# Transposing quantised activations as pairs in fp32 words, in the feed-forward phase of a decoder layer

## The chip, the core and the metric

The kernel runs on one core of one Trainium2 chip. The metric is the device time of one execution in microseconds; a kernel is given by the median of several runs.

## The reference

A decoder layer on 16 sequences of 128 tokens and 1024 channels: causal attention with rotary positions (16 heads of 64), a convolution over three neighbouring columns weighted by cosine similarities of a context, and a feed-forward part, each with a residual and a layer norm behind it. The feed-forward part is quantised: activations to integers from -128 to 127 by the row's maximum, weights to -1, 0 and 1 times a mean; its inner width is 2752.

```python
def _act_quant(x):
    scale = 127.0 / jnp.clip(jnp.max(jnp.abs(x), axis=-1, keepdims=True), EPS)
    xq = jnp.clip(jnp.round(x * scale), -128.0, 127.0) / scale
    return x + jax.lax.stop_gradient(xq - x)
...
    gate = jax.nn.silu(_bitlinear(x, w_gate))
    up = _bitlinear(x, w_up)
    return _bitlinear(gate * up, w_down)
x = _layernorm(x + _L0_attn_ref(x, L0_attn_w_q, L0_attn_w_k, L0_attn_w_v, L0_attn_w_out), axis=-1)
x = _layernorm(x + _L0_xattn_ref(x, ctx_4096, L0_xattn_weight), axis=-1)
x = _layernorm(x + _L0_ffn_ref(x, L0_ffn_w_gate, L0_ffn_w_up, L0_ffn_w_down), axis=-1)
```

## The kernel before

The kernel works in two phases, each with one turn per sequence. Phase 1 does the attention and turns the feed-forward weights into ternary fp8 values, which it stores in a DRAM scratch (`tern_dram`). Phase 2 (`turn2` of every engine) does the convolution and the feed-forward part. Between them, in phase 1's last turn, SP loads the ternary weights (lines 432 to 441): `gate8` and `up8` as 8 tiles of 128 input channels by 2752, `down8` as 22 tiles of 128 inner channels by 1024. All engines run their own hand-written order and meet at semaphores.

A turn i of phase 2, by TensorE's order (lines 711 to 747):

- The gate and up products (L717): 6 chunks of up to 512 columns, 8 matmuls for gate and 8 for up in each. The stationary operand is `xqT`, the integers of x, with channels on the partitions. ACT applies silu (L972), VectorE multiplies (L1454) and takes maxima (L1447) into `hbuf`.
- The convolution of the next sequence, 18 matmuls (L542).
- The transposes of h (L733), 22 tiles in bf16 by `idb`, in four groups `HT_USES` that take turns in two PSUM banks. h is rounded before them: ACT and VectorE add `MAGIC` to the scaled values (L978, L1466), VectorE takes it away again, limits to 127 and writes bf16 (L1472, four quarters). VectorE then evicts each group with a limit at -128 into `hT` (L1481). A group in a bank waits for the eviction of the group before it in that bank (`trh_free`).
- The down product (L745), 22 pairs of matmuls. It waits for the first two evictions before tile 0 and for the last two before tile 12. Before tile 19 come the transposes of the next x (L552), 8 tiles in bf16, which VectorE evicts into `xqT` (L1150).
- The next turn begins when `xqT` is there (`pair_free[1]`, line 712).

VectorE's order after the second eviction of h: the residual of the next x (L1133), its norm's sums (L1089 to L1094), the last two evictions of h, the norm itself (L1099), maximum and scale of x (L1082 to L1142), then, when ACT has rounded x (L784), the integers (L1146) and the eviction of `xqT` (L1150). Then it finishes the output y of this turn (L1489, L1089, L1099).

Transposes in phase 1 (L503) are in fp32 by `idf`. In the trace's names, the buffers of phase 2 are part of `weights`, and the integers of x lie in `rope_c`, y in `k`.

Of the kernel before, what the change touches and what calls it, by code (L numbers as in the profile page):

```python
# [7 lines left out]
P = 128  # L8
B, S, D = 16, 128, 1024
H, HD = 16, 64  # L10
KT = D // P
I = 2752
IT = -(-I // P)
# [28 lines left out]
HT_USES = ((0, 6), (6, 12), (12, 17), (17, 22))  # L42
HQ_NEEDS = [-(-min(hi * P, I) * 4 // I) for _, hi in HT_USES]

# [35 lines left out]
def decoder(nc, x, xT_in, ctx, wqT, wkT, wvT, woT, w_ffn, conv_w, cos, sin, causal, ident, out):  # L80
# [4 lines left out]
    with ExitStack() as stack:  # L85
# [10 lines left out]
        idb = sb("idb", [P, P], BF16)  # L96
# [31 lines left out]
        down8 = w8[:, 2 * KT * I:2 * KT * I + IT * D].rearrange("p (k n) -> p k n", k=IT)  # L128
        hbuf = over(over_out, I)
        hq = over(over_out, IT * P // 2).bitcast(BF16)  # L130
# [59 lines left out]
        xq = rope_c[:].bitcast(BF16)  # L190
# [163 lines left out]
        def _(sp):  # L354
# [38 lines left out]
            def turn(b, mode, has_next, has_next2):  # L393
# [29 lines left out]
                if has_next:  # L423
                    if not (isinstance(b, int) and b == 0):

                        sp.wait_ge(x1_stored, b * 16)
                    sp.dma_start(xres, x[bass.ds(b, 1)].rearrange("o s d -> s (o d)")).then_inc(xres_loaded, 16)
                else:

                    for w in range(2):  # L430
                        sp.wait_ge(pj_full[w], pj_uses(B - 1, 5) + 1)
                    for m, w8m in enumerate((gate8, up8)):
                        src = tern_dram[m * WCH:(m + 1) * WCH].rearrange("r p n -> (r p n)").rearrange("(k p n) -> p k n", p=P, n=I)
                        for t in (0, 4):
                            sp.dma_start(w8m[:, t:t + 4].bitcast(U8), src[:, t:t + 4]).then_inc(ffn_in, 16)
                    src = tern_dram[2 * WCH:3 * WCH].rearrange("r p n -> (r p n)").rearrange("(i n) -> i n", n=D)
                    full = (IT - 1) * P
                    src_t = src[0:full].rearrange("(k p) n -> p k n", p=P)
                    for lo, hi in ((0, 7), (7, 14), (14, IT - 1)):
                        sp.dma_start(down8[:, lo:hi].bitcast(U8), src_t[:, lo:hi]).then_inc(ffn_in, 16)  # L440
                    sp.dma_start(down8[0:I - full, IT - 1].bitcast(U8), src[full:I]).then_inc(ffn_in, 16)
# [55 lines left out]
        def _(pe):  # L497
# [48 lines left out]
            def xq_T(n, uses):  # L546
# [3 lines left out]
                bank = ps[:, 2].bitcast(BF16)  # L550
                for t in range(KT):
                    ins = nc.tensor.transpose(bank[:, t * P:(t + 1) * P], xq[:, t * P:(t + 1) * P], idb[:])  # L552
# [156 lines left out]
            def turn2(i, has_next):  # L709
# [16 lines left out]
                for u, (lo, hi) in enumerate(HT_USES):  # L726
# [4 lines left out]
                    bank = ps[:, TH + w].bitcast(BF16)  # L731
                    for t in range(lo, hi):
                        ins = nc.tensor.transpose(bank[:, (t - lo) * P:(t - lo + 1) * P], hq[:, t * P:(t + 1) * P], idb[:])  # L733
# [255 lines left out]
        def _(dve):  # L989
# [154 lines left out]
            def integers_x(n):  # L1144
                dve.wait_ge(x_rounded, n + 1)
                nc.vector.tensor_scalar(xq, xrnd, MAGIC, 127.0, ALU.subtract, ALU.min).then_inc(xq_ready, 1)  # L1146

            def xqT_out(uses):
                dve.wait_ge(pair_full[1], uses + 1)
                nc.vector.tensor_scalar(xqT, ps[:, 2].bitcast(BF16).rearrange("p (t n) -> p t n", n=P), -128.0, None,  # L1150
# [272 lines left out]
            nc.vector.tensor_copy(idb[:], idf[:]).then_inc(set_up, 1)  # L1423
# [19 lines left out]
            def turn2(i, has_next):  # L1443
# [23 lines left out]
                for a in range(4):  # L1467
# [4 lines left out]
                    nc.vector.tensor_scalar(hquarter(a, hq), hquarter(a), MAGIC, 127.0, ALU.subtract, ALU.min) \  # L1472
                        .then_inc(hq_ready, 1)
                for u, (lo, hi) in enumerate(HT_USES):
# [5 lines left out]
                    src = ps[:, TH + w].bitcast(BF16)[:, 0:(hi - lo) * P].rearrange("p (t n) -> p t n", n=P)  # L1480
                    nc.vector.tensor_scalar(hT[:, lo:hi], src, -128.0, None, ALU.max).then_inc(trh_free[w], 1)  # L1481
# [22 lines left out]
        def _(pool):  # L1504
# [31 lines left out]
            def turn(b, mode, has_next, has_next2):  # L1536
# [7 lines left out]
                if not has_next:  # L1544
# [3 lines left out]
                    nc.gpsimd.memset(down8[64:P, IT - 1], 0.0).then_inc(padded, 1)  # L1548
# [99 lines left out]
```

## Time and profile before

| | us |
|---|---|
| median of 3 runs | 1415.58 |
| lowest, highest | 1411.53, 1416.8 |
| profiled execution | 1411.78 |
| its span, first to last instruction | 1410.0 |
| TensorE busy (matmul) | 1365.8 |
| VectorE busy | 1056.1 |
| ScalarE (ACT) busy | 623.7 |
| GpSimd (POOL) busy | 217.0 |

The profile is of one execution. PE is TensorE's matmul row and PEld its weight loads, DVE is VectorE, SPq a queue of DMA issues. Busy shares are averages over both phases; phase 2 begins at 851 us. Matmuls are pipelined, so the ends of matmuls are modelled, and the starts are the ones to compare.

### The profile page before, as it was taken

The numbers are of one execution on the slowest core, as the hardware profiler recorded it, in microseconds if no ns is written. First come the engines' busy times: TensorE is split into PE (matmuls) and PEld (weight loads), VectorE is DVE, ScalarE is ACT, GpSimd is POOL, SyncE is SP. The second block draws the span as 40 slices with busy tenths as digits, with TensorE's granted clock in tenths as the row PEclk, the third lists the DMA queues.
The fourth block names the chain that finished last, engine by engine and source line by source line (L and its number), as shares of the span: only waits on it lengthen the run. The fifth ranks groups of instructions, "written<-read, shape, count | busy, mean of one in ns | idle before, by whom it ended". The sixth has DMA issues, their size and how long they took to land. (4 is left out here: it accounts for less than half of the span.)

```text
span 1410.0 us, 23306 instructions
## 1 busy us (share of the span) xinstructions
PE 1365.8 (97%) x7560; PEld 690.9 (49%) x7560; DVE 1056.1 (75%) x1851; ACT 623.7 (44%) x1209; POOL 217.0 (15%) x262
## 2 busy tenths in 40 slices
PE   8889999999999999999999989999999999999996
PEld 3344555545545554554554544444444444444443
DVE  4996456446577777868867768888888888888884
ACT  7876474455455545545544542332222232223221
POOL 0003213121131321312222221000000000000000
PEclk9999999999999999999999999999999999999999
DMA  9515454445435354453443583222222222222200
GB/s 375 223 61 181 137 186 143 168 132 182 142 111 177 137 160 141 147 178 113 159 159 124 134 278 111 76 75 74 74 74 74 74 74 74 74 74 74 77 27 16
DMA packets 63732, 178.92 MB, mean 127 GB/s; under 512 B 15392, under 2 KB 26832, under 8 KB 63696
## 3 DMA queue, kind: packets, MB, share of 16 engines
q1 hardware_dynamic: 63696, 178.48, 39.2%
q8 instruction: 18, 0.29, 0.1%
q14 instruction: 18, 0.15, 0.0%
HBM read 153.02 MB, written 25.43 MB: 127 GB/s over the span
## 5 line engine op out<-in xcount | busy, mean ns | idle before, releaser
L512 PE MATMUL ps<-weights,xT 128*128 128x512 f16 x2112 | 472.7, 381 | 7.0 <-ACT v L776 6.3
L512 PEld LDWEIGHTS ps<-weights,xT 128*128 128x128 f16 x2112 | 204.4, 98 | 243.1 <-issue 14.2
L717 PE MATMUL ps<-weights 128*128 128x512 fp8e4 (+1 forms) x1536 | 300.0, 357 | 0.0
L717 PEld LDWEIGHTS ps<-weights 128*128 128x128 bf16 x1536 | 146.7, 98 | 155.0
L512 PE MATMUL ps<-weights 128*128 128x512 f16 x768 | 168.9, 379 | 1.1 <-DVE weights L1165 0.6
L745 PE MATMUL ps<-weights 128*128 128x512 fp8e4 x704 | 157.9, 381 | 0.0
L972 ACT ACTIVATE weights<-ps,xscale 128x512 f32<-128x512 f32 x96 | 61.7, 643 | 175.7 <-PE ps L717 175.7
L832 ACT ACTIVATE prob<-prob,negmax,undo 128x128 f32<-128x128 f32 x256 | 122.7, 482 | 8.1 <-DVE negmax L1197 8.0
L512 PEld LDWEIGHTS ps<-weights 128*128 128x128 f16 x768 | 74.9, 98 | 91.8 <-DVE weights L1165 1.6
L745 PEld LDWEIGHTS ps<-weights 128*128 128x128 bf16 x704 | 67.8, 98 | 76.5 <-issue 1.1
L1529 POOL TENSOR_TENSOR rstd<-rstd,expo 128x1 f32<-128x1 f32 x32 | 17.8, 557 | 524.5 <-DVE rstd L1094 524.5
L760 ACT COPY qkT<-ps 128x512 f32<-128x512 f32 x64 | 34.3, 588 | 139.0 <-PE ps L503 139.0
L801 ACT CAST weights<-weights 128x1024 f16<-128x1024 f32 x48 | 50.2, 1045 | 68.7 <-DVE weights L1121 63.8
L809 ACT ACTIVATE wch<-wch 128x1376 f32<-128x1376 f32 x48 | 64.5, 1345 | 27.9 <-DMA wch<-w_ffn 27.8
L784 ACT ACTIVATE xT<-weights,magic,xscale 128x1024 f32<-128x1024 f32 x16 | 19.8, 1240 | 125.3 <-DVE xscale L1142 125.2
L1454 DVE SCALAR_TENSOR_TENSOR weights<-ps,xscale,weights 128x512 f32<-128x512 f32 x96 | 65.7, 685 | 7.9 <-PE ps L717 7.3
L1006 DVE SCALAR_TENSOR_TENSOR rope_c<-ps,cosb 128x512 f32<-128x512 f32 x58 | 39.7, 685 | 40.5 <-PE ps L512 31.6
L1511 POOL TENSOR_TENSOR k<-rope_c,rope_s 128x512 f32<-128x512 f32 x28 | 40.0, 1428 | 191.7 <-issue 112.8
L542 PE MATMUL ps<-weights 128*128 128x512 f16 x288 | 64.8, 379 | 1.8 <-DVE weights L1111 1.8
L1183 DVE SCALAR_TENSOR_TENSOR tern<-wch,thr,below 128x1376 fp8e4<-128x1376 f32 x24 | 52.9, 2204 | 16.5 <-ACT below L824 12.9
L1447 DVE TENSOR_REDUCE hmax<-weights 128x1 f32<-128x512 f32 x96 | 59.7, 622 | 1.2
L1126 DVE TENSOR_TENSOR weights<-weights 128x1024 f16<-128x1024 f32 x48 | 58.0, 1208 | 0.6 <-ACT weights L801 0.6
(162 smaller groups left out, 1791.0 us busy)
## 6 DMA issues: line engine op xcount, KB each, us to landing
wch<-w_ffn SPq DMA_DIRECT2D x96, 688.0 KB, 4.3
wch<-sim_scratch SPq DMA_DIRECT2D x96, 128.0 KB
ternary_scratch<-tern SPq DMA_DIRECT2D x48, 172.0 KB, 1.9
ctx<-ctx SPq DMA_DIRECT2D x16, 512.0 KB
wo_raw<-x_scratch SPq DMA_DIRECT2D x16, 512.0 KB, 3.3
out<-k SPq DMA_DIRECT2D x16, 512.0 KB, 2.7
x_in<-xT_in SPq DMA_DIRECT2D x15, 512.0 KB, 6.9
weights<-x SPq DMA_DIRECT2D x15, 512.0 KB, 10.7
```

The source lines that it names most:

```text
L512: ins = nc.tensor.matmul(ps[:, bank], partsT[:, a, t], weights[:, t, w, half * HALF:(half + 1) * HALF], start=(t == 0 and a + w == 0), sto ...
L542: ins = nc.tensor.matmul(ps[:, c], convw_parts[:, w, kk], conv_parts[:, kk, a, c * HALF:(c + 1) * HALF], start=(kk == 0 and a + w == 0), s ...
L717: ins = nc.tensor.matmul(ps[:, 2 * w + a, 0:n], xqT[:, t], w8m[:, t, at:at + n], start=(t == 0), stop=(t == KT - 1))
L745: ins = nc.tensor.matmul(ps[:, AC + c], hT[:, t], down8[:, t, c * HALF:(c + 1) * HALF], start=(t == 0), stop=(t == IT - 1))
L801: nc.scalar.copy(conv_parts[:, kk, 0], convG[:, kk + 1]).then_inc(conv_high, 1)
L809: nc.scalar.activation(wch[:, c % 2], wch[:, c % 2], ACT.Abs, accum_out=abs_part[:, bass.ds(b * SUMS + c, 1)]).then_inc(wch_free[c % 2], 1)
L832: ins = nc.scalar.activation(prob[:, r, t], prob[:, r, t], ACT.Exp, scale=undo[:, 0, 0:1], bias=negmax[:, r, t:t + 1], accum_out=rowsum[:, ...
L972: nc.scalar.activation(silu[:, w, 0:n], ps[:, 2 * w, 0:n], ACT.Silu, scale=xscale[:, 1:2]) \
L1126: nc.vector.tensor_tensor(conv_parts[:, kk, 1], convG[:, kk + 1], conv_parts[:, kk, 0], ALU.subtract) \
L1183: nc.vector.scalar_tensor_tensor(out=tern[:, c % 2], in0=wch[:, c % 2], scalar=thr[:, 0:1], in1=below[c % 2], op0=ALU.is_gt, op1=ALU.min, ...
L1447: return st.done(nc.vector.tensor_reduce(hmax[:, c:c + 1], hbuf[:, at:at + n], AX_X, ALU.max, apply_absolute_value=True))
L1454: nc.vector.scalar_tensor_tensor(out=hbuf[:, at:at + n], in0=ps[:, 2 * w + 1, 0:n], scalar=xscale[:, 2:3], in1=silu[:, w, 0:n], op0=ALU.mu ...
```

## The change

Two neighbouring integers, each with 512 added and written as fp16 (so that every 16-bit half is an ordinary number from 384 to 639), are taken as one fp32 word, and the word is transposed. 11 fp32 transposes take the place of 22 bf16 ones for h, 4 that of 8 for x, with `idf` in place of `idb`. The groups of h are 3, 3, 3 and 2 word tiles. After a transpose, a partition holds two neighbouring channels in alternate halves of its words; the eviction reads the first halves of a tile and then the second ones, takes 512 away and limits at -128. So tile t = 2j + e of `hT` and `xqT` holds the channels 2(128 j + p) + e, and the weights are loaded in the same order: each partition takes two neighbouring rows of the scratch at a time. GpSimd's padding of `down8` is 32 partitions by 2048 values instead of 64 by 1024.

```diff
--- before.py
+++ after.py
@@ -39,8 +39,10 @@
 
 SPLITS_ACT = [*range(KT, 4 * KT)]
 
-HT_USES = ((0, 6), (6, 12), (12, 17), (17, 22))
-HQ_NEEDS = [-(-min(hi * P, I) * 4 // I) for _, hi in HT_USES]
+JT = IT // 2
+LIFT = 512.0
+HT_USES = ((0, 3), (3, 6), (6, 9), (9, JT))
+HQ_NEEDS = [-(-min(hi * 2 * P, I) * 4 // I) for _, hi in HT_USES]
 
 
 def apart(eng):
@@ -93,7 +95,6 @@
 
 
         idf = sb("idf", [P, P], F32)
-        idb = sb("idb", [P, P], BF16)
         expo = sb("expo", [P, 2, 9], F32)
         wsc = sb("wsc", [P, 3], F32)
         magic = sb("magic", [P, 1], F32)
@@ -126,8 +127,12 @@
         gate8 = w8[:, 0:KT * I].rearrange("p (k n) -> p k n", k=KT)
         up8 = w8[:, KT * I:2 * KT * I].rearrange("p (k n) -> p k n", k=KT)
         down8 = w8[:, 2 * KT * I:2 * KT * I + IT * D].rearrange("p (k n) -> p k n", k=IT)
+        gate8_pairs = w8[:, 0:KT * I].rearrange("p (j m) -> p j m", j=KT // 2)
+        up8_pairs = w8[:, KT * I:2 * KT * I].rearrange("p (j m) -> p j m", j=KT // 2)
+        down8_pairs = w8[:, 2 * KT * I:2 * KT * I + IT * D].rearrange("p (j m) -> p j m", j=JT)
         hbuf = over(over_out, I)
-        hq = over(over_out, IT * P // 2).bitcast(BF16)
+        hq_pairs = over(over_out, IT * P // 2)
+        hq = hq_pairs.bitcast(F16)
         hT = over(over_out, IT * P // 2).bitcast(BF16).rearrange("p (t n) -> p t n", n=P)
         silu = over(over_out, 2 * HALF).rearrange("p (a n) -> p a n", a=2)
         if over_qkv[0] > 3 * KT * D or over_out[0] > 4 * KT * D:
@@ -187,7 +192,7 @@
         convw = tern[:].rearrange("p a n -> p (a n)").bitcast(F32)[:, 0:3 * P]
         x1p = wo_raw[:].rearrange("p a n -> p (a n)")[:, 0:D + 2]
         xres_last = wo_raw[:].rearrange("p a n -> p (a n)")[:, D + 2:2 * D + 2]
-        xq = rope_c[:].bitcast(BF16)
+        xq = rope_c[:].bitcast(F16)
         xrnd = xT[:].rearrange("p a t n -> p (a t n)").bitcast(F32)
         x2c, y = q, k
         cfit = sb("cfit", [P, 5], F32)
@@ -429,16 +434,16 @@
 
                     for w in range(2):
                         sp.wait_ge(pj_full[w], pj_uses(B - 1, 5) + 1)
-                    for m, w8m in enumerate((gate8, up8)):
-                        src = tern_dram[m * WCH:(m + 1) * WCH].rearrange("r p n -> (r p n)").rearrange("(k p n) -> p k n", p=P, n=I)
-                        for t in (0, 4):
-                            sp.dma_start(w8m[:, t:t + 4].bitcast(U8), src[:, t:t + 4]).then_inc(ffn_in, 16)
-                    src = tern_dram[2 * WCH:3 * WCH].rearrange("r p n -> (r p n)").rearrange("(i n) -> i n", n=D)
-                    full = (IT - 1) * P
-                    src_t = src[0:full].rearrange("(k p) n -> p k n", p=P)
-                    for lo, hi in ((0, 7), (7, 14), (14, IT - 1)):
-                        sp.dma_start(down8[:, lo:hi].bitcast(U8), src_t[:, lo:hi]).then_inc(ffn_in, 16)
-                    sp.dma_start(down8[0:I - full, IT - 1].bitcast(U8), src[full:I]).then_inc(ffn_in, 16)
+                    for m, w8m in enumerate((gate8_pairs, up8_pairs)):
+                        src = tern_dram[m * WCH:(m + 1) * WCH].rearrange("r p n -> (r p n)").rearrange("(j p m) -> p j m", p=P, m=2 * I)
+                        for j in (0, 2):
+                            sp.dma_start(w8m[:, j:j + 2].bitcast(U8), src[:, j:j + 2]).then_inc(ffn_in, 16)
+                    src = tern_dram[2 * WCH:3 * WCH].rearrange("r p n -> (r p n)").rearrange("(i m) -> i m", m=2 * D)
+                    full = (JT - 1) * P
+                    src_j = src[0:full].rearrange("(j p) m -> p j m", p=P)
+                    for lo, hi in ((0, 3), (3, 7), (7, JT - 1)):
+                        sp.dma_start(down8_pairs[:, lo:hi].bitcast(U8), src_j[:, lo:hi]).then_inc(ffn_in, 16)
+                    sp.dma_start(down8_pairs[0:I // 2 - full, JT - 1].bitcast(U8), src[full:I // 2]).then_inc(ffn_in, 16)
                 if has_next and not has_next2:
 
                     for w in range(2):
@@ -547,9 +552,8 @@
                 pe.wait_ge(xq_ready, n + 1)
                 if not (isinstance(uses, int) and uses == 0):
                     pe.wait_ge(pair_free[1], uses)
-                bank = ps[:, 2].bitcast(BF16)
-                for t in range(KT):
-                    ins = nc.tensor.transpose(bank[:, t * P:(t + 1) * P], xq[:, t * P:(t + 1) * P], idb[:])
+                for j in range(KT // 2):
+                    ins = nc.tensor.transpose(ps[:, 2, j * P:(j + 1) * P], rope_c[:, j * P:(j + 1) * P], idf[:])
                 ins.then_inc(pair_full[1], 1)
 
             def w_total(m):
@@ -728,9 +732,8 @@
                     if not (isinstance(i, int) and i == 0 and u < 2):
                         pe.wait_ge(trh_free[w], i * 2 + u // 2)
                     pe.wait_ge(hq_ready, i * 4 + HQ_NEEDS[u])
-                    bank = ps[:, TH + w].bitcast(BF16)
-                    for t in range(lo, hi):
-                        ins = nc.tensor.transpose(bank[:, (t - lo) * P:(t - lo + 1) * P], hq[:, t * P:(t + 1) * P], idb[:])
+                    for j in range(lo, hi):
+                        ins = nc.tensor.transpose(ps[:, TH + w, (j - lo) * P:(j - lo + 1) * P], hq_pairs[:, j * P:(j + 1) * P], idf[:])
                     ins.then_inc(trh_full[w], 1)
                 if not (isinstance(i, int) and i == 0):
                     pe.wait_ge(acc_free, i)
@@ -1143,11 +1146,12 @@
 
             def integers_x(n):
                 dve.wait_ge(x_rounded, n + 1)
-                nc.vector.tensor_scalar(xq, xrnd, MAGIC, 127.0, ALU.subtract, ALU.min).then_inc(xq_ready, 1)
+                nc.vector.tensor_scalar(xq, xrnd, MAGIC - LIFT, 127.0 + LIFT, ALU.subtract, ALU.min).then_inc(xq_ready, 1)
 
             def xqT_out(uses):
                 dve.wait_ge(pair_full[1], uses + 1)
-                nc.vector.tensor_scalar(xqT, ps[:, 2].bitcast(BF16).rearrange("p (t n) -> p t n", n=P), -128.0, None,
+                src = ps[:, 2].bitcast(F16).rearrange("p (j n e) -> p j e n", n=P, e=2)
+                nc.vector.tensor_scalar(xqT.rearrange("p (j e) n -> p j e n", e=2), src, LIFT, -128.0, ALU.subtract,
                                         ALU.max).then_inc(pair_free[1], 1)
 
             def split_w(m, tiles):
@@ -1420,7 +1424,6 @@
             w_factors(1)
             split_w(0, range(7, KT))
             dve.wait_ge(const_in, 64)
-            nc.vector.tensor_copy(idb[:], idf[:]).then_inc(set_up, 1)
             first_rope(0)
             split_w(1, range(1))
             first_rope(1)
@@ -1469,7 +1472,7 @@
                         dve.wait_ge(h_rounded, i * 2 + (a // 2 + 1))
                     elif a == 1:
                         st.wait(s)
-                    nc.vector.tensor_scalar(hquarter(a, hq), hquarter(a), MAGIC, 127.0, ALU.subtract, ALU.min) \
+                    nc.vector.tensor_scalar(hquarter(a, hq), hquarter(a), MAGIC - LIFT, 127.0 + LIFT, ALU.subtract, ALU.min) \
                         .then_inc(hq_ready, 1)
                 for u, (lo, hi) in enumerate(HT_USES):
                     w = u % 2
@@ -1477,8 +1480,9 @@
                         residual(i + 1, i * 4 + 4)
                         norm_sums(x2n)
                     dve.wait_ge(trh_full[w], i * 2 + (u // 2 + 1))
-                    src = ps[:, TH + w].bitcast(BF16)[:, 0:(hi - lo) * P].rearrange("p (t n) -> p t n", n=P)
-                    nc.vector.tensor_scalar(hT[:, lo:hi], src, -128.0, None, ALU.max).then_inc(trh_free[w], 1)
+                    src = ps[:, TH + w].bitcast(F16)[:, 0:(hi - lo) * 2 * P].rearrange("p (j n e) -> p j e n", n=P, e=2)
+                    dst = hT[:, 2 * lo:2 * hi].rearrange("p (j e) n -> p j e n", e=2)
+                    nc.vector.tensor_scalar(dst, src, LIFT, -128.0, ALU.subtract, ALU.max).then_inc(trh_free[w], 1)
                 if has_next:
                     scale_x(i * 2 + 2)
                     integers_x(i + 1)
@@ -1545,7 +1549,7 @@
                     for w in range(2):
                         pool.wait_ge(pj_full[w], pj_uses(B - 1, 5) + 1)
                     pool.wait_ge(sims_ready, b)
-                    nc.gpsimd.memset(down8[64:P, IT - 1], 0.0).then_inc(padded, 1)
+                    nc.gpsimd.memset(down8_pairs[I // 2 - (JT - 1) * P:P, JT - 1], 0.0).then_inc(padded, 1)
                     pool.wait_ge(padded, 1)
                     rstd_out(1)
                     first_rstd(b - 1)
```

On TensorE, in the loop turn of phase 2, from the semaphore of the h transposes to the loop's end. Before:

```order
L729 REGISTER_ALU
L733 MATMUL ps<-idb,weights 128x128 x12
L729 REGISTER_ALU
L733 MATMUL ps<-idb,weights 128x128 x10
L745 MATMUL ps<-weights 128x512 x24
L740 REGISTER_ALU
L745 MATMUL ps<-weights 128x512 x14
L547 REGISTER_ALU
L552 MATMUL ps<-idb,rope_c 128x128 x8
L745 MATMUL ps<-weights 128x512 x6
L751 REGISTER_ALU
```

With the change:

```order
L733 REGISTER_ALU
L736 MATMUL ps<-idf,weights 128x128 x6
L733 REGISTER_ALU
L736 MATMUL ps<-idf,weights 128x128 x5
L748 MATMUL ps<-weights 128x512 x24
L743 REGISTER_ALU
L748 MATMUL ps<-weights 128x512 x14
L552 REGISTER_ALU
L556 MATMUL ps<-idf,rope_c 128x128 x4
L748 MATMUL ps<-weights 128x512 x6
L754 REGISTER_ALU
```

The order is the same; L733 is now L736 with 6 and 5 rows for 12 and 10, L552 is L556 with 4 for 8.

On VectorE, in the same turn, from the second pair of quarters to the norm of x. Before:

```order
L1472 TENSOR_SCALAR weights<-weights 128x688 x2
L1481 TENSOR_SCALAR weights<-ps 128x768 x2
L1130 REGISTER_ALU
L1133 SCALAR_TENSOR_TENSOR weights<-ps,cfit,wo_raw 128x1024
L1089 BN_STATS stats<-weights 128x6 x2
L63 REGISTER_ALU
L1092 BN_AGGR mv<-stats 128x2
L63 REGISTER_ALU
L1094 TENSOR_SCALAR rstd<-mv 128x1
L1481 TENSOR_SCALAR weights<-ps 128x640 x2
L1099 TENSOR_SCALAR weights<-weights,mv,rstd 128x1024
```

With the change:

```order
L1475 TENSOR_SCALAR weights<-weights 128x688 x2
L1485 TENSOR_SCALAR weights<-ps 128x768 x2
L1133 REGISTER_ALU
L1136 SCALAR_TENSOR_TENSOR weights<-ps,cfit,wo_raw 128x1024
L1092 BN_STATS stats<-weights 128x6 x2
L65 REGISTER_ALU
L1095 BN_AGGR mv<-stats 128x2
L65 REGISTER_ALU
L1097 TENSOR_SCALAR rstd<-mv 128x1
L1485 TENSOR_SCALAR weights<-ps 128x768
L1485 TENSOR_SCALAR weights<-ps 128x512
L1102 TENSOR_SCALAR weights<-weights,mv,rstd 128x1024
```

Nothing moves; the last two evictions of h (L1481, now L1485) have 768 and 512 elements per partition in place of 640 and 640.

## Rows read from the trace of the kernel before

**Rows 1.** The page: busy time by engine; TensorE's granted clock in 40 slices.
```profile
PE 1365.8 (97%) x7560; PEld 690.9 (49%) x7560; DVE 1056.1 (75%) x1851; ACT 623.7 (44%) x1209; POOL 217.0 (15%) x262
...
PEclk9999999999999999999999999999999999999999
```
**Rows 2.** Timeline of a loop turn: start us, length us, engine, line, operation, count, [idle].
```profile
1079.87 0.92 PE L733 MATMUL ps<-idb,weights 128*128 128x128 bf16 x12
1080.48 1.02 DVE L1481 TENSOR_SCALAR weights<-ps 128x768 bf16<-128x768 bf16 x2
...
1081.09 0.92 PE L733 MATMUL ps<-idb,weights 128*128 128x128 bf16 x10 [0.31 <-DVE weights L1481]
...
1081.55 0.28 PEld L733 LDWEIGHTS ps<-idb,weights 128*128 128x128 bf16 x5 [0.18 <-DVE weights L1481]
...
1081.84 8.37 PE L745 MATMUL ps<-weights 128*128 128x512 fp8e4 x38
...
1084.42 0.88 DVE L1481 TENSOR_SCALAR weights<-ps 128x640 bf16<-128x640 bf16 x2
...
1089.10 0.69 DVE L1146 TENSOR_SCALAR rope_c<-xT 128x1024 bf16<-128x1024 f32 x1 [1.31 <-ACT xT L784]
...
1090.05 0.61 PE L552 MATMUL ps<-idb,rope_c 128*128 128x128 bf16 x8
...
1090.49 1.46 PE L745 MATMUL ps<-weights 128*128 128x512 fp8e4 x6
1090.69 0.69 DVE L1150 TENSOR_SCALAR weights<-ps 128x1024 bf16<-128x1024 bf16 x1 [0.90 <-PE ps L552]
...
1091.79 18.75 PE L717 MATMUL ps<-weights 128*128 128x512 fp8e4 x96
1092.15 1.28 DVE L1489 SCALAR_TENSOR_TENSOR k<-ps,hscale,q 128x1024 f32<-128x1024 f32 x1 [0.77 <-PE ps L745]
...
1126.55 1.28 DVE L1489 SCALAR_TENSOR_TENSOR k<-ps,hscale,q 128x1024 f32<-128x1024 f32 x1 [0.77 <-PE ps L745]
```
**Rows 3.** The transposes of h: what TensorE waited for (us, times).
```profile
  DVE weights L1481: 15.4, 47
```
**Rows 4.** fp32 transposes: timeline of phase 1, and the group of their weight loads.
```profile
619.61 0.60 PE L503 MATMUL ps<-idf,k 128*128 128x128 f32 x4
620.05 5.13 PE L512 MATMUL ps<-weights,xT 128*128 128x512 f16 x23
...
L503 PEld LDWEIGHTS ps<-idf,k 128*128 128x128 f32 x128 | 15.0, 141 | 0.0
```
**Rows 5.** Groups by form on VectorE: shapes, count, busy us, mean ns of one.
```profile
L1012 DVE SCALAR_TENSOR_TENSOR rope_s<-ps,sinb 128x256 f32<-128x256 f32 x116 | 43.3, 414 | 0.0
...
L1133 DVE SCALAR_TENSOR_TENSOR weights<-ps,cfit,wo_raw 128x1024 f32<-128x1024 f32 x16 | 20.4, 1275 | 2.8 <-PE ps L542 2.8
...
L1481 DVE TENSOR_SCALAR weights<-ps 128x768 bf16<-128x768 bf16 x32 | 16.2, 549 | 0.0
...
L1481 DVE TENSOR_SCALAR weights<-ps 128x640 bf16<-128x640 bf16 x32 | 14.2, 481 | 0.4 <-PE ps L733 0.3
...
L1150 DVE TENSOR_SCALAR weights<-ps 128x1024 bf16<-128x1024 bf16 x16 | 11.1, 691 | 13.5 <-PE ps L552 13.5
```
**Rows 6.** End of phase 1: timeline, and landing of the last load of L441.
```profile
839.37 3.05 SPq L441 DMA_DIRECT2D weights<-ternary_scratch  x1
...
840.61 10.53 PE L512 MATMUL ps<-weights 128*128 128x512 f16 x48 [0.44 <-DVE weights L1211]
...
DMA to landing us min/median/max: 9.4/9.4/9.4
```
**Rows 7.** Granted clock (last but two) in 2 us stretches; down product of the last turn.
```profile
1079.00:1081.00 2.00, 1.78 (x17) 1.00 (x15) 2.00 (x6) 0.48 (x1) 0.00 (x0) 1.00 0.82 186
...
1390.00:1392.00 2.00, 1.79 (x17) 1.38 (x16) 1.61 (x5) 0.00 (x0) 0.00 (x0) 0.53 0.00 0
...
1391.71 10.57 PE L745 MATMUL ps<-weights 128*128 128x512 fp8e4 x44
```

## The prediction, made before the changed kernel ran

> **What bounds the kernel now.** I began with the page: busy time by engine and the slices [rows 1]. TensorE is busy 97% of the span at full clock, VectorE 75%. That alone says that work taken from TensorE pays and that VectorE has room. But the share is an average, and all 15 phase 2 turns with a successor are alike: the same VectorE step returns after 34.40 us (1092.15 to 1126.55, [rows 2]). So I read the timeline of one such turn for the place where TensorE waits for VectorE. It has two.
>
> Place one is the hand-over of h. TensorE transposes 12 tiles from 1079.87, VectorE evicts two banks from 1080.48 to 1081.50, and only then may TensorE refill them with the other 10 tiles: the first five at 1081.09, the last five at 1081.55, the down product at 1081.84 [rows 2]. Each refill comes 0.06 us after an eviction ends. Over all turns TensorE waits for this eviction 47 times, 15.4 us in all [rows 3].
>
> Place two is the hand-over of the next x, near the end of the turn. VectorE works from the first eviction on through the sum, the norm and the other two evictions (until 1085.30) to the integers of x (L1146, ready at 1089.79); its one pause there, 1.31 us, is ACT's rounding, which is a link of the same chain. TensorE reaches the x transposes at 1090.05, having run 38 down matmuls since 1081.84. VectorE evicts xqT until 1091.38, and TensorE starts the next gate product at 1091.79, straight after its six last down matmuls [rows 2]. So VectorE is ahead here by 0.26 us and then by 0.41 us. These are thin margins: what VectorE loses beyond them, the turn loses.
>
> **TensorE's share of the change.** 22 and 8 bf16 transposes of a turn become 11 and 4 fp32 ones. The kernel already has fp32 transposes of this shape: four start at 619.61 and the product behind them at 620.05, so 0.44 / 4 = 0.11 us each [rows 4]. The eight bf16 ones of x take 1090.49 - 1090.05 = 0.44 us, 0.055 each [rows 2]. One fp32 transpose costs what two bf16 ones cost. For x the change is nil (4 x 0.11 against 0.44). For h the only transposes on the path are those behind the second eviction, the last refill: five bf16 in 1081.84 - 1081.55 = 0.29 us, now two fp32 in 0.22. That is **-0.07 us** a turn, and the whole of the gain. The rest of h's transposes run while VectorE rounds or evicts.
>
> **VectorE's share.** The evictions keep their element count (2816 for h, 1024 for x) but read PSUM with a step: the two halves of a word are neighbours in channels, and the output wants all first halves, then all second halves. The trace of before has no 16-bit read with a step, so I bound it.
> - Lower end: the price stays. 768 elements take 549 ns, 640 take 481, 1024 take 691 [rows 5]. That is 68 / 128 = 0.53 ns per element.
> - Upper end from the trace: the fp32 read of 1024 PSUM elements takes 1275 ns (L1133), 0.57 ns per element above the bf16 one. L1012 reads fp32 in PSUM at every second element: 256 in 414 ns, and (1275 - 414) / 768 = 1.12 ns per element between the two, so a step as such is not punished there [rows 5].
> - The value I take: 16-bit elements stream at twice the rate of 32-bit ones where two neighbours of the stream share a word. After the change they never do: each element comes from a word of its own, as in L1012. So I double the 0.53 ns. 768 elements: 549 + 407 = 0.96 us. 512: 549 - 136 + 271 = 0.68 us. 1024: 691 + 543 = 1.23 us.
>
> The Trainium skill, Vector Engine (DVE) Microarchitecture Reference, section 5.1, puts it as a condition: two 16-bit results per cycle need a step of one in the innermost dimension of source and destination; otherwise a PSUM read falls to one per cycle. By that rule the sum below stands; without it, by the unchanged rows, the kernel would not change. No run so far shows which.
>
> The groups change too: 768, 768, 640, 640 become 768, 768, 768, 512. Per turn VectorE then pays 0.41 + 0.41 for the first two, 0.96 - 0.48 = 0.48 for the third, 0.68 - 0.48 = 0.20 for the fourth, and 0.54 for x: **+2.04 us**. The fp16 integers that L1472 and L1146 write are as wide as the bf16 ones, from the same fp32 source, and the constants are immediates: nothing.
>
> **Where it lands.** The down product starts later by the first two evictions less the shorter last refill: 0.82 - 0.07 = **0.75 us**. The third and fourth eviction now end about 0.82 + 0.68 = 1.5 us later than 1085.30, at 1086.8. TensorE needs them after 24 down matmuls (38 take 1090.05 - 1081.84 = 8.21 us, so 5.19), at 1081.84 + 0.75 + 5.19 = 1087.8. That wait stays empty, with 1.0 us left instead of 1.7.
> The integers of x come 1.50 us late, at 1091.29, while TensorE arrives at 1090.80: a new wait of about 0.55 us in front of the x transposes. Then xqT's eviction ends 0.54 us later again, at about 1093.2, and the six down matmuls under it end at 1093.1. The gate product of the next turn starts 2.04 us late less the two margins, each less the 0.06 us of the hand-over: 2.04 - 0.20 - 0.35 = **1.49 us**.
> Behind it y (L1489) waits for the down product and follows it, so it starts no later relative to the next gate product than now, and the product and evictions of gate and up, paced by TensorE, keep their times. So 15 turns cost 15 x 1.49 = 22.4 us. The last turn has no next x and pays 0.75. Sum: **+23.1 us**.
>
> **Small things at nothing.** The eight loads of the ternary weights on SP's queue have the same bytes in runs twice as long (down rows 1 KB to 2 KB, gate and up 2.75 to 5.5 KB). The last is issued at 839.37 and lands 9.4 us later, near 848.8, while TensorE is in the 48 matmuls from 840.61 that last 10.53 us, to 851.1 [rows 6]. Longer runs could only bring it earlier; were that cover gone, and the landing later, each us would count once. POOL's memset of the padding goes from 64 x 1024 to 32 x 2048 values, twice as long, in phase 1's last turn, with nothing of SP behind it. VectorE's copy for the bf16 identity goes from the setup. xqT's eviction for the first turn is 0.54 us longer under those 48 matmuls.
>
> **The rivals.**
> 1. *The eviction keeps its two elements per step* because both halves of each word are used after all. For: the same bytes of PSUM are read. Against: the order of the stream. Then VectorE's sum is 4 x 0 for h (the regrouping moves 128 elements from the fourth group to the third) and only TensorE's -0.07 is left: 16 x -0.07 = -1.1 us, not slower, 1414.5 us. The point that decides: a growth of e in the 768-element eviction adds 2e + e + 0.67e + 1.33e = 5e to VectorE, less 0.55 of margin. 0.5% of the time, what a measurement of this kernel can tell from no change, is 7.1 us or 0.47 us a turn, so e = 0.20 us. Below an eviction of 0.75 us it is no change, above it is slower. 10%.
> 2. *Only the first place bites*: VectorE makes up its delay before the x transposes. For: VectorE is 75% busy on the page. Against: its one pause in this stretch, the 1.31 us before L1146 [rows 2], is no slack, since ACT's rounding waits for VectorE in turn. 16 x 0.75 = 12 us: 1427.6 us. 6%.
> 3. *The clock falls in the lengthened gap.* In the last turn, where no conv matmuls cover the rounding, the granted clock was 0.53 in 1390 to 1392; the 44 down matmuls from 1391.71 took 10.57 us where 44 x 0.216 = 9.5 is usual, and about 0.9 went on the half clock [rows 7]. In the common turn it stayed 1.00 over 1079 to 1081, gaps included. The gaps grow from 0.31 and 0.18 us to some 0.7 and 0.5. If it fell in every turn: 15 x 0.9 = 13.5 more, 1452 us. 7%.
> 4. *A stepped half-word read costs more than a word*, say two steps for each element: e = 1.2 us, 5 x 1.2 - 0.55 = 5.5 us a turn, 1500 us. For: no row shows such a read. Against: L1012's fp32 at a step costs nothing extra. 4%; 1% is left for what I don't name.
>
> That the change does not do what it says is hardly open: the instruction order shows 11 and 4 fp32 transposes.
>
> **The numbers.** The profiled execution took 1411.8 us (span 1410.0); 23.1 more is 1434.9. The median of the three other runs, 1415.6, lies 3.8 above it, which gives 1438.7. Two of the four executions are at the low end, so I predict **1438 us**. The main case has 72%; its own bounds (0.57 ns instead of 0.53 in every eviction, +2.5 us; fp32 transposes at the 0.141 us of their weight load [rows 4] instead of 0.11, +3; base at 1411.5, -4) give 1430 to 1444. For 8 in 10 the range takes in rival 2 and part of the way to rival 3: **1425 to 1447**. Faster than by 0.5%: 2%. Within 0.5%: 11%, rival 1 and a little. Slower: 87%.
>
> **What would show it.** In the profile after: the 768-element eviction near 0.96 us and xqT's near 1.23; the down product 0.75 us later behind the conv matmuls; a wait of TensorE's x transposes for the integers of x of about 0.5 us in 15 turns, where now there is none; a turn of 35.9 us. The forecast is wrong if the evictions stay at 0.55, or if the turn grows by 0.75 alone, or if the granted clock is below 1.00 in these gaps.

## The result, and the profile after

The changed kernel takes 1439.8 us (median of 4 runs, 1436.3 to 1443.2) against 1413.8 before (the three runs above and one more): ratio 1.0185, 95% interval 1.0166 to 1.0204. It is slower. The profiled execution took 1436.48 us, 24.7 more than the profiled one before. Each experiment below has its ratio against executions of the kernel before that ran beside it, with medians of 1411.8 to 1412.8 us. The ratios leave out four executions, two of the kernel before and two of the one with three groups, that lasted 1593 to 8152 us.

The page of the changed kernel: span, busy time, granted clock in slices. It answers to [rows 1].

```profile
span 1434.7 us, 22825 instructions
...
PE 1372.8 (96%) x7320; PEld 687.4 (48%) x7320; DVE 1088.5 (76%) x1850; ACT 623.9 (43%) x1209; POOL 219.0 (15%) x262
...
PEclk9999999999999999999999999999999999999998
```

VectorE's busy time went from 1056.1 to 1088.5, and TensorE's, with half the transposes, from 1365.8 to 1372.8. Of these 7.0 us the transposes' own rows have 2.8: 42.5 us against 39.7, since an fp32 one is booked with 293 ns where a bf16 one had 223.

The timeline of one loop turn of the changed kernel (start us, length us, engine, line, [idle before]); it answers to [rows 2]. L736 are the transposes of h, L1485 their evictions, L748 the down product, L556 and L1154 the same for x, L1149 the integers of x, L721 the gate and up product:

```profile
1088.79 1.81 DVE L1485 TENSOR_SCALAR weights<-ps 128x768 bf16<-128x768 f16 x2
...
1089.79 0.55 PE L736 MATMUL ps<-idf,weights 128*128 128x128 f32 x3 [0.68 <-DVE weights L1485]
...
1090.65 0.44 PE L736 MATMUL ps<-idf,weights 128*128 128x128 f32 x2 [0.31 <-DVE weights L1485]
...
1090.93 8.37 PE L748 MATMUL ps<-weights 128*128 128x512 fp8e4 x38
...
1093.53 1.54 DVE L1485 TENSOR_SCALAR weights<-ps 128x768 bf16<-128x768 f16 x2
...
1098.87 0.69 DVE L1149 TENSOR_SCALAR rope_c<-xT 128x1024 f16<-128x1024 f32 x1 [1.31 <-ACT xT L787]
...
1099.62 0.66 PE L556 MATMUL ps<-idf,rope_c 128*128 128x128 f32 x4 [0.33 <-DVE rope_c L1149]
...
1100.11 1.46 PE L748 MATMUL ps<-weights 128*128 128x512 fp8e4 x6
1100.32 1.23 DVE L1154 TENSOR_SCALAR weights<-ps 128x1024 bf16<-128x1024 f16 x1 [0.75 <-PE ps L556]
...
1101.69 18.75 PE L721 MATMUL ps<-weights 128*128 128x512 fp8e4 x96
...
1137.67 2.54 PE L721 MATMUL ps<-weights 128*128 128x512 fp8e4 x11
```

The two evictions last from 1088.79 to 1090.60; the refills of TensorE wait 0.68 and 0.31 us for them. The x transposes now wait 0.33 us for the integers of x. The gate product starts 0.14 us after xqT's eviction, which was not in its way before. A turn lasts 1137.67 - 1101.69 = 35.98 us instead of 34.40.

Groups by form on VectorE (count, busy us, mean ns of one), which answer to [rows 5]:

```profile
L1485 DVE TENSOR_SCALAR weights<-ps 128x768 bf16<-128x768 f16 x48 | 44.3, 950 | 0.1
...
L1154 DVE TENSOR_SCALAR weights<-ps 128x1024 bf16<-128x1024 f16 x16 | 19.6, 1224 | 11.2 <-PE ps L556 11.2
...
L1485 DVE TENSOR_SCALAR weights<-ps 128x512 bf16<-128x512 f16 x16 | 10.9, 681 | 0.0
```

And what the two kinds of transposes waited for on TensorE (us, times), of lines L736 and L556. The first answers to [rows 3]:

```profile
  DVE weights L1485: 39.0, 63
```

```profile
  DVE rope_c L1149: 17.3, 30
```

From 15.4 us the wait for the eviction of h went to 39.0, and the one for the integers of x is new. Each of these sums adds two rows of the same engine, matmuls and weight loads, that wait at the same time. On the matmuls alone the wait for the eviction of h was 4.9 us before and is 15.6 now, and the one for x is 4.9:

```profile
PE ps L736 <- DVE weights L1485: 15.6, 31, 0.7
```

The last turn: granted clock (last but two) in stretches of it, then two of a loop turn, then the down product. They answer to [rows 7]:

```profile
1412.00:1414.00 2.00, 1.36 (x7) 0.88 (x8) 2.00 (x4) 0.00 (x0) 0.00 (x0) 0.69 0.00 0
...
1416.00:1418.00 2.00, 2.00 (x6) 0.72 (x5) 0.25 (x1) 0.00 (x0) 0.00 (x0) 0.50 0.00 0
...
1088.00:1090.00 2.00, 1.32 (x10) 0.84 (x9) 2.00 (x5) 0.00 (x0) 0.00 (x0) 1.00 0.41 105
1090.00:1092.00 2.00, 1.69 (x10) 0.87 (x9) 1.97 (x3) 0.00 (x0) 0.00 (x0) 1.00 0.00 0
```

```profile
1415.10 11.88 PE L748 MATMUL ps<-weights 128*128 128x512 fp8e4 x44
```

### The profile page after: what moved, and what is told of

It reads as the page before. It is cut to its first block and busy times, and to the rows that moved or that the text cites. A ratio compares the mean times of both kernels' runs of the same rounds, so it can differ in the third digit from the quotient of the medians.

```text
span 1434.7 us, 22825 instructions
## 1 busy us (share of the span) xinstructions
PE 1372.8 (96%) x7320; PEld 687.4 (48%) x7320; DVE 1088.5 (76%) x1850; ACT 623.9 (43%) x1209; POOL 219.0 (15%) x262
## 5 line engine op out<-in xcount | busy, mean ns | idle before, releaser
L721 PE MATMUL ps<-weights 128*128 128x512 fp8e4 (+1 forms) x1536 | 300.0, 357 | 1.7
L721 PEld LDWEIGHTS ps<-weights 128*128 128x128 bf16 x1536 | 145.8, 98 | 160.0 <-issue 8.7
L748 PE MATMUL ps<-weights 128*128 128x512 fp8e4 x704 | 159.2, 383 | 0.0
L748 PEld LDWEIGHTS ps<-weights 128*128 128x128 bf16 x704 | 69.5, 99 | 77.6 <-issue 2.9
```

What stands on the lines that cost most here:

```text
L721: ins = nc.tensor.matmul(ps[:, 2 * w + a, 0:n], xqT[:, t], w8m[:, t, at:at + n], start=(t == 0), stop=(t == KT - 1))
L748: ins = nc.tensor.matmul(ps[:, AC + c], hT[:, t], down8[:, t, c * HALF:(c + 1) * HALF], start=(t == 0), stop=(t == IT - 1))
```

## The experiments

A turn is measured between the starts of two gate products in the loop (34.40 us before).

**The stepped read alone.**

```diff
-                    src = ps[:, TH + w].bitcast(BF16)[:, 0:(hi - lo) * P].rearrange("p (t n) -> p t n", n=P)
-                    nc.vector.tensor_scalar(hT[:, lo:hi], src, -128.0, None, ALU.max).then_inc(trh_free[w], 1)
+                    src = ps[:, TH + w].bitcast(BF16)[:, 0:(hi - lo) * P].rearrange("p (n e) -> p e n", e=2)
+                    dst = hT[:, lo:hi].rearrange("p t n -> p (t n)").rearrange("p (e n) -> p e n", e=2)
+                    nc.vector.tensor_scalar(dst, src, -128.0, None, ALU.max).then_inc(trh_free[w], 1)
```

(xqT's eviction in the same way.)

> The kernel before with its bf16 transposes, its groups of 6, 6, 5 and 5 tiles and its loads, but with evictions of h and x that read PSUM at every second 16-bit element (so the channels come out in a wrong order). Theory S (the stepped read on VectorE's chain is the whole cost): the 768-element eviction takes 0.95 us, the 640-element one 0.82, x's 1.23; a turn grows by about 1.6 us, the time by 24 us, ratio 1.016 to 1.020. Theory T (the fp32 transposes on TensorE are the cost): the time stays, ratio 1.000.

Measured: 1437.1 us, ratio 1.0180 (1.0155 to 1.0205). Its groups on VectorE:

```profile
L1483 DVE TENSOR_SCALAR weights<-ps 128x768 bf16<-128x768 bf16 x32 | 29.1, 952 | 0.1
...
L1483 DVE TENSOR_SCALAR weights<-ps 128x640 bf16<-128x640 bf16 x32 | 24.8, 816 | 0.0
...
L1151 DVE TENSOR_SCALAR weights<-ps 128x1024 bf16<-128x1024 bf16 x16 | 19.6, 1224 | 10.7 <-PE ps L552 10.7
```

And two gate products of its timeline:

```profile
1104.10 18.75 PE L717 MATMUL ps<-weights 128*128 128x512 fp8e4 x96
...
1140.06 5.12 PE L717 MATMUL ps<-weights 128*128 128x512 fp8e4 x23
```

The turn is 35.96 us. Nothing of the change is in this kernel but the order in which VectorE reads PSUM, and it has the change's whole cost. Theory T falls.

**All of the change but the stepped read.**

```diff
-                src = ps[:, 2].bitcast(F16).rearrange("p (j n e) -> p j e n", n=P, e=2)
-                nc.vector.tensor_scalar(xqT.rearrange("p (j e) n -> p j e n", e=2), src, LIFT, -128.0, ALU.subtract,
-                                        ALU.max).then_inc(pair_free[1], 1)
+                src = ps[:, 2].bitcast(F16).rearrange("p (t n) -> p t n", n=P)
+                nc.vector.tensor_scalar(xqT, src, LIFT, -128.0, ALU.subtract, ALU.max).then_inc(pair_free[1], 1)
...
-                    src = ps[:, TH + w].bitcast(F16)[:, 0:(hi - lo) * 2 * P].rearrange("p (j n e) -> p j e n", n=P, e=2)
-                    dst = hT[:, 2 * lo:2 * hi].rearrange("p (j e) n -> p j e n", e=2)
+                    src = ps[:, TH + w].bitcast(F16)[:, 0:(hi - lo) * 2 * P].rearrange("p (t n) -> p t n", n=P)
+                    dst = hT[:, 2 * lo:2 * hi]
```

> The changed kernel with both evictions reading PSUM in storage order, so that the two channels of a word stay side by side and the products use wrong channels; fp32 transposes, the added 512, groups and loads stay. Theory S: evictions back at 0.55, 0.42 and 0.69 us, the turn back at 34.4 us, ratio to before 0.998 to 1.002. Theory T: ratio stays near 1.018.

Measured: 1412.9 us, ratio 1.0004 (0.9992 to 1.0016). Its groups, and its timeline:

```profile
L1484 DVE TENSOR_SCALAR weights<-ps 128x768 bf16<-128x768 f16 x48 | 25.1, 550 | 0.6 <-PE ps L736 0.6
...
L1154 DVE TENSOR_SCALAR weights<-ps 128x1024 bf16<-128x1024 f16 x16 | 11.1, 691 | 13.0 <-PE ps L556 13.0
```

```profile
1092.58 18.75 PE L721 MATMUL ps<-weights 128*128 128x512 fp8e4 x96
...
1126.95 18.25 PE L721 MATMUL ps<-weights 128*128 128x512 fp8e4 x90
```

fp16 for bf16, the second operation (subtract, then max) and the fp32 transposes leave the evictions at 0.55 and 0.69 us. The turn is 34.37 us: transposing in words neither costs nor gains.

**h alone, and x alone.** The first has the change's lines for h and those of before for x, the second the other way round.

> The change made for h alone (transposes, eviction, down weights); x as before. Theory S: the delay of VectorE's chain is 1.50 us at the integers of x, less the margin of about 0.2 us: a turn grows by 1.3 us, the time by 20 to 21 us, ratio 1.014 to 1.015. A rival, that only the delay of the down product (0.78 us) counts: 12 us, ratio 1.009.

> The change made for x alone; h as before. Theory S: the eviction of x grows by 0.53 us against a margin of 0.35 us, a turn grows by 0.2 to 0.3 us, the time by 3 to 5 us, ratio 1.002 to 1.004. Rivals: the 0.53 us count whole, 8 us, 1.006; or the margin hides them, 1.000. With h alone it should add up to the whole change.

Measured: h 1433.6 us, ratio 1.0144 (1.0127 to 1.0161); x 1418.3 us, ratio 1.0032 (1.0016 to 1.0049). Gate products of the first:

```profile
1103.67 18.75 PE L723 MATMUL ps<-weights 128*128 128x512 fp8e4 x96
...
1139.35 5.99 PE L723 MATMUL ps<-weights 128*128 128x512 fp8e4 x27
```

and of the second:

```profile
1098.87 18.75 PE L719 MATMUL ps<-weights 128*128 128x512 fp8e4 x96
...
1133.53 11.81 PE L719 MATMUL ps<-weights 128*128 128x512 fp8e4 x54
```

Turns of 35.68 and 34.66 us: +1.28 and +0.26, together 1.54 of the 1.58. The parts add to within 0.04 us. With x alone the margin of the trace before is seen at work: xqT's eviction grew by 0.53 us (to 1224 ns, as in the change), the turn by 0.26. With h alone the rival of 12 us falls.

**Only the late evictions stepped, and only the early ones.** In the first, the first two evictions of h read in storage order, and the third, the fourth and x's stay stepped; in the second, it is the other way round. The edit to the eviction of h in the first:

```diff
+                    src = ps[:, TH + w].bitcast(F16)[:, 0:(hi - lo) * 2 * P]
+                    dst = hT[:, 2 * lo:2 * hi]
+                    if u < 2:
+                        src = src.rearrange("p (t n) -> p t n", n=P)
+                    else:
+                        src = src.rearrange("p (j n e) -> p j e n", n=P, e=2)
+                        dst = dst.rearrange("p (j e) n -> p j e n", e=2)
```

> The changed kernel with the first two evictions of h reading PSUM in storage order (channels in these groups are then wrong); the third, the fourth and x's stay stepped. Theory S, by the two margins: the integers of x come 0.66 us late, less 0.2, and x's eviction 0.53, less 0.35: a turn grows by 0.65 to 0.8 us, 10 to 12 us in all, ratio 1.007 to 1.009. The rival that the evictions TensorE does not wait for at once (the third and fourth, needed at tile 12 only) are hidden: only x's counts, as with x alone, ratio 1.003.

> The changed kernel with only the first two evictions of h stepped; the third, the fourth and x's read in storage order (channels in these are then wrong). Theory S: the down product starts 0.78 us later, VectorE's chain is 0.81 us late at the integers of x, less than that start plus the margin, so TensorE's own delay is what is left: a turn grows by 0.75 to 0.85 us, 12 to 14 us in all, ratio 1.008 to 1.010. The rival that the margins absorb part of it as they did for the late evictions: ratio 1.004 to 1.006.

Measured: late 1423.7 us, ratio 1.0072 (1.0049 to 1.0094), turn 35.18 us; early 1426.3 us, ratio 1.0107 (1.0078 to 1.0136), turn 35.17 us. So +0.78 and +0.77, together 1.55 of the 1.58. Of the late ones' 0.78 us, x's eviction has 0.26 by the experiment before, which leaves 0.52 for the third and fourth of h. The timeline of the first:

```profile
1085.70 1.01 DVE L1490 TENSOR_SCALAR weights<-ps 128x768 bf16<-128x768 f16 x2
...
1087.04 8.37 PE L748 MATMUL ps<-weights 128*128 128x512 fp8e4 x38
...
1094.98 0.69 DVE L1149 TENSOR_SCALAR rope_c<-xT 128x1024 f16<-128x1024 f32 x1 [1.31 <-ACT xT L787]
...
1095.73 0.66 PE L556 MATMUL ps<-idf,rope_c 128*128 128x128 f32 x4 [0.33 <-DVE rope_c L1149]
```

The down product starts as early as with plain evictions (1087.04 - 1085.70 = 1.34 us after the start of the first one, 1.36 in [rows 2]), and yet the x transposes wait, until 1095.67, for the integers of x. The third and fourth evictions delay no matmul that reads them: they end at 1091.18, and the 25th down matmul comes 5.19 us after the first, at 1092.2. They delay the norm of x behind them on VectorE. The rival (hidden) falls. The early ones delay TensorE at once: in the second kernel's trace the down product starts 2.14 us after the first eviction, as in the change, and no margin helps.

**The step on TensorE's side.** The evictions as in the second experiment, the weights in the change's order, and

```diff
+        xq_halves = xqT.rearrange("p t n -> p (t n)").rearrange("p (j n e) -> p j e n", n=P, e=2)
+        h_halves = hT.rearrange("p t n -> p (t n)").rearrange("p (j n e) -> p j e n", n=P, e=2)
...
-                            ins = nc.tensor.matmul(ps[:, 2 * w + a, 0:n], xqT[:, t], w8m[:, t, at:at + n],
+                            ins = nc.tensor.matmul(ps[:, 2 * w + a, 0:n], xq_halves[:, t // 2, t % 2], w8m[:, t, at:at + n],
...
-                        ins = nc.tensor.matmul(ps[:, AC + c], hT[:, t], down8[:, t, c * HALF:(c + 1) * HALF],
+                        ins = nc.tensor.matmul(ps[:, AC + c], h_halves[:, t // 2, t % 2], down8[:, t, c * HALF:(c + 1) * HALF],
```

> The changed kernel with evictions in storage order and the step moved to TensorE: the stationary operands of the gate, up and down products read every second element of xqT and hT. Everything is computed. If the weight load keeps its 98 ns: turn 34.4 us, ratio 0.998 to 1.001 as with plain evictions. Rival: a stepped weight load is slower; up to some 200 ns it stays under the 216 ns of a 512-column matmul, but under the 192-column ones (16 a turn, 80 ns each) it shows: at 200 ns 16 x 0.1 = 1.6 us a turn or more, ratio 1.02.

Measured: 1412.8 us, ratio 0.9992 (0.9979 to 1.0006), turn 34.36 us. The weight loads of the gate and up product:

```profile
L724 PEld LDWEIGHTS ps<-weights 128*128 128x128 bf16 x1536 | 147.0, 98 | 154.7
```

They keep their 98 ns with every second element read. This kernel computes all that the change computes and has none of its cost; nor does it gain.

**Three groups instead of four**, in the kernel before and on top of the last one.

```diff
-HT_USES = ((0, 6), (6, 12), (12, 17), (17, 22))
+HT_USES = ((0, 8), (8, 16), (16, 22))
...
-                    if t in (0, 12):
-                        for w in range(2):
-                            pe.wait_ge(trh_free[w], i * 2 + (1 if t == 0 else 2))
+                    if t in (8, 16):
+                        pe.wait_ge(trh_free[t // 8 % 2], i + 1 if t == 8 else i * 2 + 2)
```

> The kernel before with three groups of h (8, 8 and 6 tiles) in place of four, so that the down product waits for one eviction and the six transposes behind it instead of two evictions: its start comes about 0.28 us earlier, VectorE's chain is shorter by one fixed part (0.06 us), and the margin of 0.2 us at the integers of x takes just that: turn 34.1 to 34.2 us, 3 to 4 us less in all, ratio 0.997 to 0.998. Rival: VectorE's chain sets the turn and the gain is eaten by a wait at the x transposes, ratio 1.000.

> The stationary step together with three groups of 4, 4 and 3 word tiles. If both hold: as the kernel before with three groups, ratio 0.997 to 0.998; if the stepped weight load costs, that cost less 3 to 4 us.

Measured: 1412.2 us, ratio 0.9993 (0.9979 to 1.0008), turn 34.48 us; and 1415.6 us, ratio 1.0030 (1.0005 to 1.0054), turn 34.52 us. No gain, and the second is slower by 0.3%; the forecast of 0.997 to 0.998 missed for both. The first one's timeline:

```profile
1116.04 1.29 DVE L1482 TENSOR_SCALAR weights<-ps 128x1024 bf16<-128x1024 bf16 x2
...
1116.79 0.51 PE L733 MATMUL ps<-idb,weights 128*128 128x128 bf16 x6 [0.34 <-DVE weights L1482]
...
1117.13 8.36 PE L746 MATMUL ps<-weights 128*128 128x512 fp8e4 x38
...
1120.26 0.55 DVE L1482 TENSOR_SCALAR weights<-ps 128x768 bf16<-128x768 bf16 x1
...
1121.01 0.81 DVE L1100 TENSOR_SCALAR weights<-weights,mv,rstd 128x1024 f32<-128x1024 f32 x1 [0.20 <-POOL rstd L1530]
...
1124.90 0.69 DVE L1147 TENSOR_SCALAR rope_c<-xT 128x1024 bf16<-128x1024 f32 x1 [1.31 <-ACT xT L785]
```

The down product does start earlier (1.09 us after the first eviction, 1.36 in [rows 2]), but L1147, the integers of x, comes 8.86 us after it instead of 1089.10 - 1080.48 = 8.62. Two evictions of 1024 now stand ahead of the residual, 1.29 us in place of 1.02; and the third no longer fills the time in which VectorE waits for GpSimd's rstd, so 0.20 us of idle time stand before L1100. The rival of the expectation held, by a mechanism it didn't name.

**ACT takes evictions**: the second of h and x's in the changed kernel, the second of h in the kernel before.

```diff
+                act.wait_ge(trh_full[1], i * 2 + 1)
+                src = ps[:, TH + 1].bitcast(F16)[:, 0:(hi - lo) * 2 * P].rearrange("p (j n e) -> p j e n", n=P, e=2)
+                dst = hT[:, 2 * lo:2 * hi].rearrange("p (j e) n -> p j e n", e=2)
+                nc.scalar.activation(dst, src, ACT.Identity, bias=unlift[:, 0:1]).then_inc(trh_free[1], 1)
```

> The changed kernel, steps kept, with ACT taking the second eviction of h and x's (without the limit at -128, which the scale by the row's maximum never lets act). ACT evicts 512 fp32 elements from PSUM in 588 ns in the kernel before. If a stepped 16-bit read costs ACT no more than one element per cycle: 0.8 us for 768 and 1.0 us for 1024, the turn grows by 0.5 us instead of 1.6, ratio 1.005 to 1.007. If the stepped read is slow for any engine that reads PSUM (each twice as long): 1.6 and 2.0 us, the turn grows by 1.5 us or more, ratio 1.017.

> The kernel before with ACT taking the second eviction of h beside VectorE's first (again without the limit at -128). Both places in TensorE's turn should gain: the down product starts 0.2 us earlier, VectorE's chain is 0.47 us shorter. Turn 34.2 us, 3 us in all, ratio 0.998. Rival: ACT's eviction takes over 0.9 us and the start is no earlier, ratio 1.000.

Measured: 1420.5 us, ratio 1.0056 (1.0036 to 1.0076), turn 35.00 us; and 1416.6 us, ratio 1.0028 (1.0014 to 1.0042), turn 34.51 us. ACT's groups in the first:

```profile
L993 ACT ACTIVATE weights<-ps,unlift 128x1024 bf16<-128x1024 f16 x15 | 16.7, 1113 | 22.2 <-PE ps L557 22.2
L988 ACT ACTIVATE weights<-ps,unlift 128x768 bf16<-128x768 f16 x16 | 14.4, 901 | 21.7 <-PE ps L737 21.7
```

Stepped reads of 768 and 1024 cost ACT 0.90 and 1.11 us; in the second, the plain read of 768 costs it 0.80. The two also differ in the operation (bias or copy), so how much of the 0.10 us between them is the step's was not parted. But ACT's time per element is the same with and without it: (1113 - 901) / 256 = 0.83 ns stepped, and (798 - 588) / 256 = 0.82 between its plain 16-bit copy of 768 and its fp32 copies of 512 in the kernel before. It had no doubled rate to lose. About two thirds of the change's cost goes that way. In the kernel before there was nothing to win, and the forecast of 0.998 missed, as its timeline shows:

```profile
1112.73 0.55 DVE L1487 TENSOR_SCALAR weights<-ps 128x768 bf16<-128x768 bf16 x1
1113.06 0.80 ACT L982 COPY weights<-ps 128x768 bf16<-128x768 bf16 x1 [1.33 <-PE ps L733]
...
1113.34 1.04 PE L733 MATMUL ps<-idb,weights 128*128 128x128 bf16 x10 [0.31 <-DVE weights L1487]
...
1114.21 8.37 PE L745 MATMUL ps<-weights 128*128 128x512 fp8e4 x38
```

ACT's eviction starts 0.33 us after VectorE's, since its six tiles are transposed later, and ends at 1113.86, 1.13 us after the start of the first one, where VectorE's second one ended after 1.02. The down product starts 1.48 us after the first eviction, not 1.36. No version here beats the kernel before by more than its interval.

## Why the prediction was right

**The eviction's price**, the one unknown, was taken at twice the time per element: 0.96, 0.68 and 1.23 us. Measured 0.950, 0.681 and 1.224. The argument was the row of L1012 (a step alone costs fp32 nothing) and the doubled rate of neighbouring halves. The first two experiments show it from both sides: with the step 1.018, without it 1.000. Per element it is (950 - 681) / 256 = 1.05 ns in the changed kernel and (550 - 414) / 256 = 0.53 in the second experiment, whose 512-element evictions took 414 ns. The rule quoted from the Trainium skill, Vector Engine (DVE) Microarchitecture Reference, section 5.1, that a read from PSUM without a step of one falls from two elements per cycle to one, agrees with this factor of two.

**Where it lands.** Counted from the start of the first eviction, the down product came at 2.14 us instead of 1.36: +0.78, predicted 0.75. The integers of x ended at 10.77 instead of 9.31: +1.46, predicted 1.50. The gate product came at 12.90 instead of 11.31: +1.59, predicted 1.49. The last two fp32 transposes of h took 1090.93 - 1090.65 = 0.28 us, not 0.22, so TensorE's gain was 0.01 and not 0.07. That moved only the start of the down product, which waits for x later anyway; it is no term of the turn. On the turn's path VectorE's chain was 0.04 us better than predicted, and two terms were short. The four transposes of x took 0.49 us and not 0.44: in the second experiment, where they wait for nothing, they take 0.44 (1090.85 to 1091.29 in its trace), and here they stand behind a wait. And from the end of xqT's eviction to the gate product passed 0.14 us, where I had carried over the 0.06 us of another hand-over. The second margin was thus 0.41 - 0.14 = 0.27 us, which fits x alone: 0.53 - 0.27 = 0.26. The wait at the x transposes had been announced as 0.55 us; the trace shows 0.33 on the matmuls, but 1099.62 against the arrival at 1090.93 + 8.21 = 1099.14 is 0.48.

**The sum.** From the first gate product of phase 2 to the last, 15 turns: 1389.60 - 849.70 = 539.90 us, against 1366.92 - 850.98 = 515.94 before, +24.0 (predicted 22.4). The last turn to the end: 45.1 against 43.1, +2.0 (predicted 0.75). Phase 1 ended 1.3 us earlier. Together 24.7 against 23.1 predicted. The last turn was under-sized: the granted clock, which I put only to a rival, stayed lower for longer there. Its down product took 11.88 us against 10.57 in [rows 7], 1.3 us more. In the kernel with h alone it took 10.81 and in the first experiment 10.61 with much the same gaps, so its size does not follow from the gaps alone, and why the clock stayed down for longer here wasn't tried. The rest of the last turn's +2.0 us is the 0.71 us by which its down product started later. The 1.3 us of phase 1 are not the change's, as far as the traces tell: in the thirteen traces phase 2 begins between 848.1 and 856.2 us, while the turns of each agree within 0.1 us. So the change cost 24.0 + 2.0 = 26.0 us, as the medians have it (1439.8 - 1413.8), against 23.1 predicted. That 1438 came so near to 1439.8 is in part luck: the base that I added to was 1.8 us too high.

**The small things** cost nothing that is seen. GpSimd's memset took 1.80 us (0.95 before). The last load of the weights, issued at 833.69 by the trace, landed 13.1 us later at 846.8, still under the 48 matmuls; it took longer from issue to landing than the 9.4 us in [rows 6], so nothing here shows that longer runs made it faster. The 48 matmuls of the last projection still took 10.53, and the gate product followed them at once:

```profile
DMA to landing us min/median/max: 13.1/13.1/13.1
...
816.26 1.80 POOL L1552 MEMSET weights<- 32x2048 fp8e4 x1
...
839.33 10.53 PE L517 MATMUL ps<-weights 128*128 128x512 f16 x48 [0.36 <-DVE weights L1215]
...
849.70 2.54 PE L721 MATMUL ps<-weights 128*128 128x512 fp8e4 x11
```

**The rivals.** The first (no loss of rate) fell with the evictions' times. The second (only the down product's delay) fell with the turn of h alone. The third (the clock in the loop) fell with the windows, at 1.00 in the gaps of the loop turn, and with the turns of the trace, 35.98 to 36.05 us each. The fourth (a step that costs more than a word) fell with 0.950 us. The four runs lie in two pairs, near 1436.4 and near 1443.2, and their mean granted clock is 0.994 and 0.993 in the faster pair, 0.990 and 0.988 in the slower. In which stage the clock was lower there is open, since only the first was traced. The prediction also reads the 15.4 us of [rows 3] as what TensorE waited for the eviction; that sum has both rows, and the matmuls waited 4.9 us. No term of its sum rests on it.

## What to carry to other kernels

A transposition in wider words saves TensorE little where one fp32 transpose costs two bf16 ones, and it leaves the interleaving to someone; look at who undoes it, and on which path. An operation on VectorE that runs at twice the rate on 16-bit elements from PSUM (0.53 ns each here) lost it with a step of two in the source (1.05 ns); other steps were not run. Here the same step in a stationary operand was free, and on ACT nearly so. Margins are to be read at each hand-over: 0.26 and 0.41 us of them turned a delay of 2.0 us into 1.6, and evictions that no matmul waits for still cost where TensorE waits for what the same engine does next (0.52 us a turn here).

## What the hardware showed that was not expected

Weight loads of 128 x 128 bf16 with every second element kept 98 ns. ACT reads stepped 16-bit elements from PSUM in 0.90 us for 768, so it is faster there than VectorE's 0.950, while for a plain read VectorE's 0.549 beats ACT's 0.80.
